# Attention block of a convolution network: the second 1x1 convolution from half-precision high and low parts

## What is computed

```python
small = bilinear_resize(x, 64, 64)
a     = relu(bn1(conv1x1(small, w1)))                 # 256 channels
q, k  = conv1x1(a, wq, bq), conv1x1(a, wk, bk)        # 32 channels each
v     = conv1x1(a, wv, bv)
att   = softmax(q^T k) applied to v                   # 4096 x 4096 weights per image
h     = relu(bn2(gamma * att + a))
y     = bn3(conv1x1(h, w2))                           # "the second convolution"
out   = relu(bilinear_resize(y, 128, 128) + x)
```

## Time and profile before

| | |
|---|---|
| median of 3 runs | 2367.95 us (2367.91 to 2372.15) |
| the profiled execution | 2371.97 us |
| its span, first to last instruction | 2370.2 us |
| TensorE clock granted, mean | 0.994 of full |
| busy share of the span | PE 97%, DVE 75%, ACT 72%, POOL 70% |
| DMA | 204.11 MB, mean 86 GB/s |

### The profile page before, as it was taken

One profiled execution on the slowest core, in us unless ns is written; L12 is line 12 of the kernel. 1 busy time (PEld: TensorE's weight loads), 2 busy tenths in 40 slices (PEclk: granted clock), 3 DMA queues, 4 the chain that ended last, 5 costly groups with the idle time before them and its releaser, 6 DMA issues.

```text
span 2370.2 us, 48197 instructions
## 1 busy us (share of the span) xinstructions
PE 2298.5 (97%) x15970; PEld 1650.3 (70%) x15970; DVE 1783.7 (75%) x3294; ACT 1706.3 (72%) x3305; POOL 1671.0 (70%) x1610
## 2 busy tenths in 40 slices
PE   4799999999999999999999999999999999999998
PEld 2377777777667777777747777777775777777774
DVE  7666578887568888888657888888756777777778
ACT  5567777777657777777755777777765777777773
POOL 7992468888369988888728988889845454444464
PEclk8899999999999999999999999999999999999999
DMA  6321112322102332222301322233310112222322
GB/s 212 107 72 46 36 54 107 106 92 104 54 23 103 108 107 103 93 105 98 107 10 54 109 106 102 102 107 106 106 55 1 63 63 71 71 71 71 142 96 100
DMA packets 59273, 204.11 MB, mean 86 GB/s; under 512 B 8752, under 2 KB 9840, under 8 KB 59120
## 3 DMA queue, kind: packets, MB, share of 16 engines
q1 hardware_dynamic: 41696, 138.93, 18.2%
q10 hardware_dynamic: 17424, 63.45, 6.5%
HBM read 135.24 MB, written 67.11 MB: 85 GB/s over the span
## 4 chain that ended last, share of the span: by engine, by line
PE 88%; DVE 4%; ACT 3%; POOL 3%; issue 1%; SPq 1%; DMA 0%; DVEq 0%; ACTq 0%; POOLq 0%
PE acc L1139 19%; PE acc L1141 18%; PE acc L1140 18%; PE et L1015 10%; PE emx L1003 6%; PE wrk L1037 4%; PE acc L1065 4%; PE wrk L1003 3%; PE acc L1057 2%; PE wrk L1028 1%; DVE qs L768 1%; DVE ks L768 1%; PE acc L1049 1%; ACT qs L535 1%; ACT qs L534 1%
## 5 line engine op out<-in xcount | busy, mean ns | idle before, releaser
L1139 PE MATMUL acc<-vh,ph 128*128 128x257 f16 x4096 | 1120.1, 273 | 1.7 <-DVE vl L778 1.4
L1141 PE MATMUL acc<-vh,pl 128*128 128x257 f16 x4096 | 1116.2, 273 | 0.0
L1140 PE MATMUL acc<-vl,ph 128*128 128x256 f16 x4096 | 1110.9, 271 | 0.0
L463 ACT ACTIVATE ph<-et 128x512 f16<-128x512 f32 x1024 | 610.5, 596 | 301.8 <-PE et L1015 293.0
L727 DVE TENSOR_TENSOR pl<-et,ph 128x512 f16<-128x512 f32 x1024 | 700.6, 686 | 139.4 <-ACT et L464 135.8
L464 ACT ACTIVATE et<-et 128x512 f32<-128x512 f32 x1024 | 607.0, 593 | 0.0
L1140 PEld LDWEIGHTS acc<-vl,ph 128*128 128x128 f16 x4096 | 400.9, 98 | 277.4 <-issue 20.5
L1139 PEld LDWEIGHTS acc<-vh,ph 128*128 128x128 f16 x4096 | 400.2, 98 | 70.6 <-issue 11.0
L1141 PEld LDWEIGHTS acc<-vh,pl 128*128 128x128 f16 x4096 | 395.4, 97 | 56.2
L377 POOL TENSOR_TENSOR ct<-cd,uw 128x512 f32<-128x512 f32 x246 | 325.0, 1343 | 134.7 <-DVE xres L758 130.3
L1015 PE MATMUL et<-qs,ks 98*128 (+1 forms) x1024 | 390.2, 381 | 2.7 <-DVE pl L727 0.9
(11 more groups left out here) (142 smaller groups left out, 2673.0 us busy)
## 6 DMA issues: line engine op xcount, KB each, us to landing
xres<-in_x SPq DMA_DIRECT2D x139, 512.0 KB, 4.5
out<-xres ACTq DMA_DIRECT2D x121, 512.0 KB, 2.6
xin<-in_x SPq DMA_DIRECT2D x110, 512.0 KB, 3.7
xr<-in_x SPq DMA_DIRECT2D x7, 512.0 KB, 7.4
out<-xr SPq DMA_DIRECT2D x6, 512.0 KB, 2.6
out<-xr SPq DMA_DIRECT2D x2, 256.0 KB, 2.1
osb<-in_L_conv_conv_w SPq DMA_DIRECT2D x1, 256.0 KB, 7.7
osb<-in_L_conv_v_w SPq DMA_DIRECT2D x1, 256.0 KB, 7.8
```

What stands on the lines that cost most here:

```text
L463: ops.activation(ph[:, t % 4, :], et[t % 2][:, :], ACT.Exp)
L1139: mm(acc[it][:, 0:C + 1], ph[:, tt % 4, pt], vh[:, tt, 0:C + 1], start=tt == 0, stop=False)
L1140: mm(acc[it][:, 0:C], ph[:, tt % 4, pt], vl[:, tt, :], start=False, stop=False)
L1141: last = mm(acc[it][:, 0:C + 1], pl[:, tt % 4, pt], vh[:, tt, 0:C + 1], start=False, stop=tt == JT - 1)
```

## The change

`conv2` no longer multiplies float32 by float32. The weights are divided once by the largest absolute weight of their input channel and split into half precision parts `w2h` and `w2l`; `h` is scaled by a number that is derived once a batch from a bound (so that it fits half precision), and split into `hh` and `hl`. Each float32 product becomes three half-precision products: `w2h*hh`, `w2h*hl`, `w2l*hh`. ACT now makes `hh` (`high_h`, where `relu_h` stood) and, in steps of its own, the same rectified value in float32 (`relu_h`, steps `T_RELU`); DVE subtracts them (`low_h`, steps `T_LOW`). `T_CV` moves from (20, 22) to (21, 23), `T_CV_LAST` from (9, 11) to (11, 13), and one pair of units moves from step 24 to step 20. The scales come from small DVE instructions and, once a batch after step 29 of its first chunk, from two float32 products of a 128 x 128 matrix of ones with one column each (for the first batch two more, with two columns each). bn3 undoes the scale.

```diff
+        hh = sb("hh", [P, CH, IB], F16)
+        hl = sb("hl", [P, CH, IB], F16)
+        w2h = sb("w2h", [P, CH, C], F16)
+        w2l = sb("w2l", [P, CH, C], F16)
...
-        ones_d = sb("ones_d", [D, P])
+        ones_p = sb("ones_p", [P, P])
...
+            def high_h(chunk, half):
+                act.wait_ge(ot_done, chunk * 2 + (half + 1))
+                act.wait_ge(h_scaled, chunk // NB + 1)
+                at_least(act, cv_rdy, chunk * 2)
+                ops.activation(hh[:, half, :], hbuf[:, half, :], ACT.Relu, bias=h_par[:, 1, half:half + 1],
+                               scale=h_par[:, 0, half:half + 1]).then_inc(hh_rdy, 1)
+
             def relu_h(chunk, half):
-                act.wait_ge(ot_done, chunk * 2 + (half + 1))
-                ops.activation(hbuf[:, half, :], hbuf[:, half, :], ACT.Relu, bias=par[:, B2, half:half + 1],
-                               scale=par[:, S2, half:half + 1]).then_inc(h_rdy, 1)
+
+                act.wait_ge(hh_rdy, chunk * 2 + (half + 1))
+                ops.activation(hbuf[:, half, :], hbuf[:, half, :], ACT.Relu, bias=h_par[:, 1, half:half + 1],
+                               scale=h_par[:, 0, half:half + 1]).then_inc(h_rdy, 1)
...
                             for half in range(2):
+                                high_h(b * NB - 1, half)
                                 relu_h(b * NB - 1, half)
...
                     if c > 0 and t in (T_OT[0] + 2, T_OT[1] + 2):
-                        relu_h(g - 1, T_OT.index(t - 2))
+                        high_h(g - 1, T_OT.index(t - 2))
+                    t_relu = T_RELU_LAST if is_last(b, c) else T_RELU
+                    if c > 0 and t in t_relu:
+                        relu_h(g - 1, t_relu.index(t))
...
             for half in range(2):
+                high_h(NB * B - 1, half)
                 relu_h(NB * B - 1, half)
...
+            def low_h(chunk, half):
+
+                dve.wait_ge(h_rdy, chunk * 2 + (half + 1))
+                ops.tensor_tensor(hl[:, half, :], hbuf[:, half, :], hh[:, half, :], ALU.subtract).then_inc(hl_rdy, 1)
...
+                    for h in range(CH):
+                        ops.tensor_scalar(w2h[:, h, :], w2t[:, h, :], w2_inv[:, h:h + 1], None, ALU.mult).then_inc(h_fixed, 1)
...
+                    for h in range(CH):
+                        last = ops.scalar_tensor_tensor(w2l[:, h, :], w2t[:, h, :], w2_inv[:, h:h + 1], w2h[:, h, :], ALU.mult,
+                                                        ALU.subtract)
+                    last.then_inc(w2_rdy, 1)
...
+                    if g == 0 and t in T_FIXED_H:
+                        fixed_sizes_of_h(T_FIXED_H.index(t))
+                    if c == 0 and t == T_PART_H:
+                        part_of_h(b)
+                    if c == 0 and t > T_SUM_H:
+                        size_of_h(b, t - T_SUM_H - 1)
+                    if c == 1 and t < 2:
+                        size_of_h(b, t + 2)
+                    t_low = T_LOW_LAST if is_last(b, c) else T_LOW
+                    if g > 0 and t in t_low:
+                        low_h(g - 1, t_low.index(t))
...
             residual(NB * B - 1, NB - 1, 0)
             residual(NB * B - 1, NB - 1, 1)
+            low_h(NB * B - 1, 0)
+            low_h(NB * B - 1, 1)
             add_piece(0, LATE - 1, 2)
             add_piece(0, LATE - 1, 3)
...
             def conv2(chunk, half):
-                pe.wait_ge(h_rdy, chunk * 2 + 2)
+                pe.wait_ge(hl_rdy, chunk * 2 + 2)
...
                 for h in range(CH):
-                    last = mm(bank[:, :], w2t[:, h, half * P:(half + 1) * P], hbuf[:, h, :], start=h == 0, stop=h == CH - 1)
+                    mm(bank[:, :], w2h[:, h, cs], hh[:, h, :], start=h == 0, stop=False)
+                    mm(bank[:, :], w2h[:, h, cs], hl[:, h, :], start=False, stop=False)
+                    last = mm(bank[:, :], w2l[:, h, cs], hh[:, h, :], start=False, stop=h == CH - 1)
...
+                    if c == 0 and t == T_SUM_H:
+                        pe.wait_ge(h_part_rdy, b + 1)
+                        pe.wait_ge(m_rdy, g + 2)
+                        for h in range(CH):
+                            last = mm(wrk[:, 0:1], ones_p[:, :], h_part[:, h:h + 1], start=h == 0, stop=h == CH - 1)
+                        last.then_inc(h_sum, 1)
+                        if is_first(b):
+                            pe.wait_ge(h_fixed_rdy, 1)
+                            for h in range(CH):
+                                last = mm(wrk[:, 1:3], ones_p[:, :], h_parts[:, h, :], start=h == 0, stop=h == CH - 1)
+                            last.then_inc(h_fixed_sum, 1)
...
-T_CV = (20, 22)
+T_CV = (21, 23)
+T_RELU = (6, 10)
+T_LOW = (19, 20)
+T_RELU_LAST = (4, 8)
+T_LOW_LAST = (6, 9)
+T_FIXED_H = (3, 5, 7, 8, 10, 11)
+T_PART_H = 13
+T_SUM_H = 29
...
-    _k = 0 if _t == 0 else 2 if _t in (9, 12, 15, 18, 19, 24, 25) else 1
+    _k = 0 if _t == 0 else 2 if _t in (9, 12, 15, 18, 19, 20, 25) else 1
...
-T_CV_LAST = (9, 11)
+T_CV_LAST = (11, 13)
```

More of the change, by code:

```diff
@@ L36 @@
 BN = 1.0 / (1.0 + 1e-5) ** 0.5
+H_TOP = 2.0 ** 14
 HUGE = 3.4028234663852886e38
@@ L68, in attention_block_kernel @@
         hbuf = sb("hbuf", [P, CH, IB])
+        hh = sb("hh", [P, CH, IB], F16)
+        hl = sb("hl", [P, CH, IB], F16)
+        w2h = sb("w2h", [P, CH, C], F16)
+        w2l = sb("w2l", [P, CH, C], F16)
+        hs = sb("hs", [P, 18])
+        w2_max, w2_inv, s2_abs, b2_abs, h_scale, h_fix = (hs[:, 2 * i:2 * i + 2] for i in range(6))
+        h_var, h_all, h_inv, gam_abs = (hs[:, i:i + 1] for i in range(12, 16))
+        h_part = sb("h_part", [P, CH])
+        h_parts = sb("h_parts", [P, CH, 2])
+        h_par = sb("h_par", [P, 3, CH])
         win = sb("win", [P, 2, CH, BR + 2, S])
@@ L132, in attention_block_kernel @@
         ot_rdy, ot_done, h_rdy = sem("ot_rdy"), sem("ot_done"), sem("h_rdy")
+        h_fixed, h_fixed_rdy, h_fixed_sum, w2_rdy = (sem(n) for n in ("h_fixed", "h_fixed_rdy", "h_fixed_sum", "w2_rdy"))
+        h_part_rdy, h_sum, h_step, h_scaled, hh_rdy, hl_rdy = (
+            sem(n) for n in ("h_part_rdy", "h_sum", "h_step", "h_scaled", "hh_rdy", "hl_rdy"))
         cv_rdy, y_rdy = sem("cv_rdy"), sem("y_rdy")
@@ L390, in _ @@
             pool.wait_ge(mem_ok, 4)
-            ops.memset(ones_d[:], 1.0).then_inc(mem_ok, 1)
+            ops.memset(ones_p[:], 1.0).then_inc(mem_ok, 1)
             pool.wait_ge(mem_ok, 5)
@@ L494, in bn3 @@
                 for dst, src in jobs + [(new[:, 1:BR + 1, :], cv)]:
-                    done = ops.activation(dst, src, ACT.Identity, bias=par[:, B3, half:half + 1], scale=par[:, S3, half:half + 1])
+                    done = ops.activation(dst, src, ACT.Identity, bias=par[:, B3, half:half + 1], scale=h_par[:, 2, half:half + 1])
                 done.then_inc(y_rdy, 1)
@@ new lines, in part_of_h, with size_of_h @@
+            def part_of_h(b):
+                if b == 0:
+                    dve.wait_ge(h_fixed_rdy, 1)
+                ops.tensor_tensor(h_part[:], am1[:], h_parts[:, :, 0], ALU.mult).then_inc(h_part_rdy, 1)
+            def size_of_h(b, part):
+                if part == 0:
+                    dve.wait_ge(h_sum, b + 1)
+                    if b == 0:
+                        dve.wait_ge(h_fixed_sum, 1)
+                        ops.tensor_scalar(h_fix, wrk[:, 1:3], 1e-30, None, ALU.max).then_inc(h_fixed, 1)
+                        dve.wait_ge(h_fixed, 9)
+                        ops.tensor_tensor(h_fix[:, 0:1], h_fix[:, 0:1], gam_abs, ALU.mult).then_inc(h_fixed, 1)
+                        dve.wait_ge(h_fixed, 10)
+                    ops.tensor_scalar(h_var, h_fix[:, 0:1], vg[:, 0:1], h_fix[:, 1:2], ALU.mult, ALU.add).then_inc(h_step, 1)
+                    dve.wait_ge(h_step, b * 4 + 1)
+                    ops.tensor_scalar(h_all, wrk[:, 0:1], h_var, None, ALU.add).then_inc(h_step, 1)
+                elif part == 1:
+                    dve.wait_ge(h_step, b * 4 + 2)
+                    ops.reciprocal(h_inv, h_all).then_inc(h_step, 1)
+                    ops.tensor_scalar(h_par[:, 2, :], par[:, S3, :], h_all, 1.0 / H_TOP, ALU.mult, ALU.mult)
+                elif part == 2:
+                    dve.wait_ge(h_step, b * 4 + 3)
+                    ops.tensor_scalar(h_scale, w2_max, h_inv, H_TOP, ALU.mult, ALU.mult).then_inc(h_step, 1)
+                else:
+                    dve.wait_ge(h_step, b * 4 + 4)
+                    ops.tensor_tensor(h_par[:, 0, :], h_scale, par[:, S2, :], ALU.mult)
+                    ops.tensor_tensor(h_par[:, 1, :], h_scale, par[:, B2, :], ALU.mult).then_inc(h_scaled, 1)
@@ L968, in _ @@
             pe.wait_ge(size_part, 1)
-            mm(acc[3][:, 4 * D:4 * D + 2], ones_d[:, :], ws[:, :], start=True, stop=True).then_inc(size_sum, 1)
+            mm(acc[3][:, 4 * D:4 * D + 2], ones_p[0:D, :], ws[:, :], start=True, stop=True).then_inc(size_sum, 1)
             pe.wait_ge(wt_ok, 3)
@@ L1035, in conv2 @@
                     pe.wait_ge(y_rdy, chunk * 2 + 1)
```

(9 more changed lines are left out.)

19 lines of the change are left out of this document (added).

## The result

The changed kernel takes 2365.95 us (median of 20 runs, 2364.95 to 2368.55), the kernel before 2368.95 us (20 runs, 2367.91 to 2372.15). The ratio is 0.9987, its 95% interval 0.9981 to 0.9993: faster by 3.0 us, 0.13%, less than the 0.2% of the prediction. Forecast were 15.8 us, and 2352.2 us with 2345 to 2364 as the range: the time lies outside.

The account below looks back on a forecast made before the run. PE, busy 97% of the span, was taken as the bound. Terms -26.0 + 3.0 + 2.0 + 1.0 + 1.0 + 3.2 = -15.8 us took 2367.95 to 2352.2 us; range 2345 to 2364 us for 8 in 10.

Parts of the forecast that it names:

- What DVE gains: Prediction's part on DVE's added work: `low_h` 1.0 us over all chunks, small instructions 1.0 us, chunk 0 nothing.
- The layout: Steps 19 to 21 of chunk 3: both `low_h` done at 365.1, PE at `conv2` at 365.29, 0.1 to 0.2 us spare.
- the list of signs: What the profile after would show, among it `low_h` near 0.85 and 0.68 us and `hl` waits about 1 us.
- the third rival: At step 21 `conv2` waits for low parts that POOL slows: up to 34 us, so +17 us, 2385 us; chance 0.11.
- The second rival: DVE bounds the full chunks, taking back 0.84 us in each of 18: -0.7 us, 2367.2 us; chance 0.10.
- PE, 62 halves: `conv2` halves in 31 of 32 chunks go from 1.72 to 1.30 us on PE: 26.0 us saved.
- `low_h` and `conv2`'s wait: PE's wait at `conv2` for the low parts from DVE: 1.0 us over all chunks, from 0 to 34 us.
- the three entries: Entries of batches 1 to 3: two more ACT instructions delay the first keys by 0.67 us each, 2.0 us in all.
- sums and small instructions: One-column products on PE, 20 at 0.15 us, 3.0 us; small DVE instructions 0.25 us a batch, 1.0 us.
- last chunk, low parts beside the adds: Last chunk: its `conv2` lies in the tail, where DVE leads, and was counted at nothing.
- tail: After the last step two `low_h` precede DVE's adds, which come 3.2 us later (1.5 to 4).
- the moved steps: `conv2` one step later, two in the last chunk, so POOL's piece starts later: nothing; uncovered about 2 us, once.

Follow-up runs that it names:

- the experiment on this chunk: Changed kernel with the last chunk's low parts at steps (7, 10) and the adds of its second and third piece spread later: 2363.62 us.
- the kernel before again: The kernel before the change, unedited, timed and profiled a second time: 2370.38 us, ratio 1.0001 to the kernel before.
- the early low parts: Changed kernel with `T_LOW` (18, 19) in place of (19, 20), nothing else: 2350.77 us, ratio 0.992.
- the copy with one: Changed kernel with `hl` made by a plain copy of the float32 value in place of the subtraction, so the output differs: 2358.27 us.
- the version with the other order: Changed kernel with DVE's tail reordered: last two add parts first, then first `low_h`, late differences, second `low_h`, late weighting: 2365.86 us.

## Why the prediction was wrong

The step that failed is in "What DVE gains": "So I take 0.85 us for `low_h(0)` and 0.75 us for `low_h(1)`", and with it "I put 1.0 us on it over all chunks". The layout was right (DVE just free for its maximum, no idle time, 0.1 to 0.2 us to spare); the two durations were 0.6 us too short in sum. They turned the room into a wait of 0.51 us, that is 7.1 us in 14 chunks, and small delays behind it make 9.8. For `low_h(0)` I used an add beside the two products L365, 0.83 us; `low_h` itself took 1.00 us beside the same two (L379 now). That was the wrong way to set a price: the add had started 0.33 us into the first product and waited only for its short rest, `low_h` would start 0.18 us into it. For `low_h(1)` I looked at no neighbour (and wrote 0.75 us in the layout, 0.68 in the list of signs). The same view of before had it, one row below:

```profile
363.46 1.26 POOL L370 TENSOR_TENSOR y<-win,rt 128x512 f32<-128x512 f32 x1
364.80 1.02 POOL L372 TENSOR_TENSOR cd<-y 128x504 f32<-128x504 f32 x1
```

My `low_h(1)` ran from 364.4 to 365.1, across both; measured beside these two instructions: 1.24 us. Priced by turns, the rows of before give the miss: `low_h(0)` takes 0.99 us and puts off the second L365 until 363.83; L370 then runs to 365.17, `low_h(1)` ends at 365.72, and PE, due at 365.29, waits 0.4 us. That is an estimate from the earlier trace rows, the row L370 and the 0.14 us of the section on the result. This is the third rival's mechanism, to which I gave 0.11, at the place that it named; it cost 8.8 us more than forecast and not 33, since it hit 14 chunks and not 18, by 0.7 us and not by 1.9. The rival's own threshold, a wait of 0.9 us in 18 chunks, was not reached, so the change stayed just faster. The second rival has nearly the right time (2367.2 us), by luck and for a wrong reason: the same DVE work one step earlier costs nothing.

The terms one by one, forecast and then measured between the profiled executions:

| term | forecast | measured |
|---|---|---|
| PE, 62 halves | -26.0 | -26.0 (0.84 us a chunk, wherever nothing waits) |
| `low_h` and `conv2`'s wait | +1.0 | +9.8 |
| the three entries | +2.0 | +2.5 |
| sums and small instructions | +4.0 | +1.7 |
| last chunk, low parts beside the adds | 0 | +2.4 |
| tail | +3.2 | +3.3 |
| start, chunk 0 | 0 | +0.35 |
| sum | -15.8 | -6.0, and the times differ by 6.0 |

- *Sums.* The products with one column, in after, x4 being a group:

```profile
198.92 0.50 PE L1277 MATMUL wrk<-h_part,ones_p 128*128 128x1 f32 x4
199.28 0.59 PE L1282 MATMUL wrk<-h_parts,ones_p 128*128 128x2 f32 x4
199.73 0.27 PE L1245 MATMUL acc<-vh,ph 128*128 128x257 f16 x1
```

  0.36 us for the four with one column, 0.45 for the four with two, so 0.09 and 0.11 each, at the lower bound that the earlier trace rows gave; I took 0.15. Between one, two and (in the transposes of the earlier trace rows) 128 columns the distance hardly differs. With the small DVE instructions, taken as what the first two chunks of a batch lack of their 0.84 us each, it is 0.9 us in the first batch, 0.2 in the next two and 0.36 in the last.
- *The last chunk.* "Nothing; uncovered about 2 us, once" stands in the text under the moved steps, but for POOL's piece. The cost came from DVE (2.1 of the 2.4 us, which the experiment on this chunk gave back; the other 0.3 arise at the end of the chunk before, and I did not look for their cause): I had laid out `low_h` against PE in an ordinary chunk, never against the adds of the last one, where the table puts it between adds of neighbouring steps.
- *The entries.* Each got 0.75 us more of PE's wait (1.72 against 0.97), not 0.67: four separate instructions pass over ACT in 3.10 us, where two had taken 1.51 together.
- *The median.* The pair of profiles gives 6.0 us, the medians 3.0. The profiled execution of before lies 3.0 us above its median (2371.97 against 2368.95), that of after at its own. Scatter of 1.7 to 1.8 us was seen in the entry of batch 2, where the clock fell (the kernel before again, and the early low parts). The first execution kept its clock there, so where it had its 3 us stays open. I had carried the difference of two medians over as if it were a constant.

The Trainium skill (GPSIMD Engine Reference, Specifications) names the contention between GpSimd and DVE instructions with two SBUF inputs. I cited it, and then used the milder of the durations that the trace offered. The runs agree that there is contention (0.69 us alone, 1.00 and 1.24 beside POOL). They do not show that it takes two inputs: the copy with one went from 0.42 to 0.73 and 0.86 us at the same places.

## What to carry to other kernels

Where a forecast of a wait rests on a few tenths of room, lay the new instruction's window over the other engine's rows one by one. Beside POOL its price is its own time plus the rest of what runs when it starts; beside which instruction a similar one was once seen says little. If the room is smaller than the spread of that price, give the wait its own chance. An instruction that feeds a wait belongs where its result is a step early: here one step earlier was worth 15.2 us, and one step later cost some 30. Special stretches (entries, the last chunk, the tail) have tables of their own and need a layout of their own; here they cost 8.2 us of a saving of 26.

## What the runs showed of the hardware

**DVE and POOL take turns, and lock in a pattern.** A subtraction of 512 columns took 0.69 us alone and up to 1.67 beside POOL; POOL's products beside it went from 1.19 to 1.64 us for two. The one that starts second pays: it waits for the rest of the other's instruction (less 0.14 us) and then takes its usual time. So it was in all 275 `low_h` that got longer, also where `low_h` was a copy with one SBUF input, and 481 of the 484 adds of 512 columns (L755 and L758) of the kernel before take what this sum gives, to 0.04 us. Beside POOL's L364 `low_h` kept its 0.69 us and POOL took 1.22 for 0.73, since `low_h` was first. The pattern repeats from chunk to chunk, mostly to 0.03 us in one execution; between executions of the same instructions most chunks agree to 0.1 us and single ones differ by up to 0.26. So the cost of a place is nearly a fixed number.

**The clock fell in the tail, and at times in an entry.** PE stood still for 4.54 us in front of `conv2`. PE in after:

```profile
2329.68 0.41 PE L1141 MATMUL wrk<-hh,w2h 128*128 128x512 f16 x1 [4.54 <-DVE hl L771]
2329.90 0.61 PE L1142 MATMUL wrk<-hl,w2h 128*128 128x512 f16 x1
2330.31 0.63 PE L1143 MATMUL wrk<-hh,w2l 128*128 128x512 f16 x1
```

Windows of after; the granted clock stands behind the busy times:

```profile
2328.00:2330.00 2.00, 0.32 (x2) 0.21 (x3) 1.14 (x3) 0.86 (x2) 0.00 (x0) 0.98 0.56 225
2330.00:2332.00 2.00, 2.00 (x6) 0.64 (x5) 1.97 (x5) 0.00 (x0) 0.00 (x0) 0.50 0.09 37
```

The products come 0.43 us apart instead of 0.22: 0.50 is the lower of the two levels, 1.2 GHz. Before the change PE stood still for only 2.10 us at this place, and there the clock stayed at 1.00 in one profile and fell to 0.50 in the other (the kernel before again, from 2340 to 2342 us). The gap at the return of the batch loop is like that: 1.79 us before and 1.93 in after with the clock at 1.00, 1.92 and 2.00 in two other executions with the clock at 0.50 behind it, which cost 1.7 us. So a short gap may or may not cost the clock. In after the fall in the tail cost nothing, since DVE led; in the version with the other order DVE waited 0.95 us for the second half of `conv2`.
